# The second of fourteen FFN blocks by seven products instead of plainly, with its weights prepared inside the attention

## The reference

```python
xn = _layernorm(x, axis=-1)                       # x: (2, 512, 512) float32
s = attention(xn, wq, wk, wv, wo)                 # 32 query heads, 8 key heads, window 128
gate_proj = (gate_w - rep(gate_z)) * rep(gate_s)  # (512, 1792), groups of 128 rows; up_proj alike
down_proj = (down_w - rep(down_z)) * rep(down_s)  # (1792, 512)
g = _silu((_silu(xn @ gate_proj) * (xn @ up_proj)) @ down_proj)
return x + s * g
```

## Time and profile before

| | us |
|---|---|
| median of three runs | 873.48 |
| the profiled execution | 873.48 |
| its span, first to last instruction | 871.0 |
| PE busy | 861.2 (99%) |
| DVE busy | 674.5 (77%) |
| POOL busy | 577.2 (66%) |
| ACT busy | 493.5 (57%) |
| mean granted clock of PE | 0.999 of full |
| FFN's first matmul | 663.78 |

### The profile page before, as it was taken

One profiled execution on the slowest core, in us unless ns is written; L12 is line 12 of the kernel. 1 busy time (PEld: TensorE's weight loads), 2 busy tenths in 40 slices (PEclk: granted clock), 3 DMA queues, 4 the chain that ended last, 5 costly groups with the idle time before them and its releaser, 6 DMA issues.

```text
span 871.0 us, 14447 instructions
## 1 busy us (share of the span) xinstructions
PE 861.2 (99%) x4340; PEld 725.6 (83%) x4340; DVE 674.5 (77%) x1264; ACT 493.5 (57%) x1322; POOL 577.2 (66%) x500
## 2 busy tenths in 40 slices
PE   8999999999999999999999999999999999999997
PEld 7888888888888888888888888888888888888886
DVE  8877777877686877877776877778665888989876
ACT  5766565655656566656556555665564444444443
POOL 4665566666675776667666757764446887888865
PEclk9999999999999999999999999999999999999999
DMA  8111110131003012100311020116374564655542
GB/s 263 38 49 37 36 39 25 26 97 36 25 14 106 24 36 90 30 24 24 96 36 36 24 85 24 36 48 159 85 212 120 144 179 132 177 150 167 161 133 96
DMA packets 94851, 72.25 MB, mean 83 GB/s; under 512 B 4192, under 2 KB 80480, under 8 KB 94816
## 3 DMA queue, kind: packets, MB, share of 16 engines
q1 hardware_dynamic: 94096, 70.70, 27.6%
q10 hardware_dynamic: 720, 1.11, 0.4%
HBM read 63.41 MB, written 8.39 MB: 82 GB/s over the span
## 4 chain that ended last, share of the span: by engine, by line
PE 91%; DVE 5%; ACT 2%; DMA 1%; POOL 1%; issue 1%; SPq 0%; DVEq 0%
PE ps L38 29%; PE ps L39 29%; PE ps L40 29%; PE ps L1099 3%; PE ps L1079 1%; ACT probs L1242 1%; DMA work<-L_attn_wv 1%; DVE ps L1507 1%; DMA y<-L_attn_x 0%; DVE work L1503 0%; DVE work L1502 0%; DVE work L1509 0%; POOL w_lo L983 0%; POOL pt_lo L1373 0%; DVE xt_lo L1471 0%
## 5 line engine op out<-in xcount | busy, mean ns | idle before, releaser
L38 PE MATMUL ps<-xt_hi,w_lo 128*128 128x512 f32 x412 | 164.5, 399 | 0.4 <-POOL w_lo L209 0.4
L39 PE MATMUL ps<-xt_lo,w_hi 128*128 128x512 f32 x412 | 161.5, 392 | 0.0
L40 PE MATMUL ps<-xt_hi,w_hi 128*128 128x512 f32 x412 | 160.7, 390 | 0.0
L1373 POOL TENSOR_TENSOR pt_lo<-kept,pt_hi 128x512 fp32r<-128x512 f32 x112 | 142.8, 1293 | 24.9 <-ACT pt_hi L1253 24.6
L1368 POOL TENSOR_TENSOR q_lo<-work,q_hi 128x512 fp32r<-128x512 f32 x63 | 81.3, 1292 | 90.9 <-ACT q_hi L1225 90.9
L1242 ACT ACTIVATE probs<-ps,neg_max 128x128 f32<-128x128 f32 x256 | 90.7, 366 | 42.8 <-DVE neg_max L1527 42.8
L1253 ACT ACTIVATE pt_hi<-kept 128x512 fp32r<-128x512 f32 x112 | 69.2, 633 | 65.6 <-DVE kept L1540 65.6
L38 PE MATMUL ps<-wo_hi,o_lo 128*128 (+1 forms) x256 | 99.8, 390 | 0.1
L40 PE MATMUL ps<-wo_hi,o_hi 128*128 (+1 forms) x256 | 99.6, 389 | 0.0
L39 PE MATMUL ps<-wo_lo,o_hi 128*128 (+1 forms) x256 | 99.6, 389 | 0.0
L40 PEld LDWEIGHTS ps<-xt_hi,w_hi 128*128 128x128 f32 x412 | 77.5, 188 | 17.4
(11 more groups left out here) (174 smaller groups left out, 2234.7 us busy)
## 6 DMA issues: line engine op xcount, KB each, us to landing
work<-L_attn_wq SPq DMA_DIRECT2D x32, 256.0 KB, 2.8
work<-L_attn_wo SPq DMA_DIRECT2D x32, 256.0 KB, 2.7
work<-L_ffn_gate_w SPq DMA_DIRECT2D x14, 256.0 KB, 3.7
work<-L_ffn_gate_z SPq DMA_DIRECT2D x14, 256.0 KB, 4.6
work<-L_ffn_gate_s SPq DMA_DIRECT2D x14, 256.0 KB, 5.8
work<-L_ffn_up_w SPq DMA_DIRECT2D x14, 256.0 KB, 2.9
work<-L_ffn_up_z SPq DMA_DIRECT2D x14, 256.0 KB, 4.0
work<-L_ffn_up_s SPq DMA_DIRECT2D x14, 256.0 KB, 4.5
```

Source lines behind the costliest of these rows:

```text
L38: pe.matmul(out, stat[1], mov[0], start=first, stop=False, skip_group_check=grown)
L39: pe.matmul(out, stat[0], mov[1], start=False, stop=False, skip_group_check=grown)
L40: return pe.matmul(out, stat[0], mov[0], start=False, stop=last, skip_group_check=grown)
L1373: pool.tensor_tensor(pt_lo[:, w, :], kept[:, w, :], pt_hi[:, w, :].bitcast(F32), ALU.subtract).then_inc(pt_split, 1)
```

## The change

- The second block of pair 0 is made by seven products too: `BLOCKS` = 13, `FIRST_BLOCK` = 1, and blk = 0 is now that block. The old numbering moves on by one. Its 48 plain matmuls are replaced by 42.
- blk = 0 has no down products between its own (pair 0 has nothing before it). Its order is U1, U2, S2, S1, S3, G2, S4, and G2 goes to a bank of its own (D = bank 4, a bank that the down products use later), with no wait for the third copy; DVE adds the copy there (`add_gate1`), then ACT takes the silu.
- The last unit of the attention prepares other pieces: down of block 0 at (1, 0), in the row of the token sums' buffer (`first_down`), up of block 1 at (1, 1) and (1, 2), gate at (1, 2), and POOL's `lo_gate(0)` with ACT's two `hi_s` at (1, 3). Before, gate, up and down at (1, 0) to (1, 2).
- ACT's list for blk = 0 is: copy 0, copy 1, hi_up(1), copy 2, hi_gate(1), hi_s(1, 0), silu_gate2, silu_gate1, hi_s(1, 1), hi_down(0). DVE's is: dequantise up(1), add_up1, dequantise gate(1), add_gate2, add_gate1, dequantise down(0).
- At blk = 1 PE waits for the two silus of blk 0 before its first down product.

```diff
-IN_BODY = [(GATE, 1, 0), (UP, 1, 0), (DOWN, 0, 0), (UP, 0, 1), (GATE, 0, 1), (DOWN, 1, 0)]
+IN_BODY = [(DOWN, 0, 0), (UP, 1, 0), (GATE, 1, 0), (UP, 0, 1), (GATE, 0, 1), (DOWN, 1, 0)]
-SEVEN_FROM = 1
-BLOCKS = 2 * (PAIRS - SEVEN_FROM)
+FIRST_BLOCK = 1
+BLOCKS = NI - FIRST_BLOCK
...
-    A, B, C = (0, 3), 1, 2
+    A, B, C, D = (0, 3), 1, 2, 4
...
     def products(self, pe, blk, downs):
...
+        def fifth():
+            if blk:
+                pe.wait_ge(self.seven_mid, 2 * blk)
+            else:
+                pe.wait_ge(sh.silu_done, 2)
+            self.product(pe, blk, S1, self.C, True, self.t_of(T1))
+
+        def sixth():
+            pe.wait_ge(self.copied, 3 * blk + 1)
+            self.product(pe, blk, S2, a, False, self.t_of(T2))
+
+        pe.wait_ge(self.s_split, 2 * blk + 2)
         if blk:
-            pe.wait_ge(self.seven_mid, 2 * blk)
+            fifth()
+            sixth()
         else:
...
+            sixth()
+            fifth()
+
+        if blk == 1:
+
+            pe.wait_ge(self.seven_silu, 2)
...
-        pe.wait_ge(self.copied, 3 * blk + 3)
-        self.product(pe, blk, G2, a, False, self.t_of(T4))
+        if blk:
+            pe.wait_ge(self.copied, 3 * blk + 3)
+            self.product(pe, blk, G2, a, False, self.t_of(T4))
+        else:
+            self.product(pe, blk, G2, self.D, True, self.t_of(T4))
         pe.wait_ge(self.added, 3 * blk + 2)
...
+    def add_gate1(self, dve):
+
+        dve.wait_ge(self.made, self.DONE_P4)
+        dve.wait_ge(self.copied, 3)
+        dve.tensor_tensor(self.bank(self.D), self.bank(self.D), self.copies[:, 2, :], ALU.add).then_inc(self.gate1_added, 1)
...
     def silu_gate1(self, act, blk):
-        act.wait_ge(self.made, 7 * blk + self.DONE_P4)
+        if blk:
+            act.wait_ge(self.made, 7 * blk + self.DONE_P4)
+        else:
+            act.wait_ge(self.gate1_added, 1)
...
-            for e in range(EARLY_PRODUCTS, 4):
-                gate_up(0, e)
             for blk in range(BLOCKS):
+                n, ii = pair_of(blk)
                 def downs(which):
                     for t in which:
-                        down(SEVEN_FROM + blk // 2, 4 * (blk % 2) + t)
+
+                        if n:
+                            down(n, 4 * ii + t)
...
-            sv.hi_up(act, 0)
 
             act.wait_ge(sh.y_ready, NKV * TT)
-            hi_of_mid(0, *ORDER[0])
-            hi_of_mid(0, *ORDER[1])
-            sh.silu(act, 0, 2)
-            sv.hi_gate(act, 0)
-            sv.hi_s(act, 0, 0)
-            sv.hi_s(act, 0, 1)
-            hi_of_mid(0, *ORDER[2])
-            sv.hi_down(act, -1)
-            sh.silu(act, 0, 3)
-            hi_of_mid(0, *ORDER[3])
+            hi_of_mid(0, 0, 0)
+            hi_of_mid(0, 0, 1)
...
+                if blk == 0:
+
+                    sv.copy(act, blk, 1)
+                    sv.hi_up(act, 1)
+                    sv.copy(act, blk, 2)
+                    sv.hi_gate(act, 1)
+                    sv.hi_s(act, 1, 0)
+                    sv.silu_gate2(act, blk)
+                    sv.silu_gate1(act, blk)
+                    sv.hi_s(act, 1, 1)
+                    sv.hi_down(act, blk)
+                    continue
...
-            sv.lo_up(pool, 0)
-            split_mid(0, *ORDER[0])
-            split_mid(0, *ORDER[1])
-            sv.lo_gate(pool, 0)
-            split_mid(0, *ORDER[2])
-            sv.lo_down(pool, -1)
-            split_mid(0, *ORDER[3])
+            split_mid(0, 0, 0)
+            split_mid(0, 0, 1)
...
                 sv.dequantise(dve, blk + 1, GATE)
-                accumulate(n, 4 * ii)
-                accumulate(n, 4 * ii + 1)
-                sv.dequantise(dve, blk, DOWN)
+                for t in (0, 1) if n else ():
+                    accumulate(n, 4 * ii + t)
+                if blk:
+                    sv.dequantise(dve, blk, DOWN)
                 sv.add_gate2(dve, blk)
-                accumulate(n, 4 * ii + 2)
-                accumulate(n, 4 * ii + 3)
+                if blk == 0:
+                    sv.add_gate1(dve)
+                    sv.dequantise(dve, blk, DOWN)
+                for t in (2, 3) if n else ():
+                    accumulate(n, 4 * ii + t)
...
-        FFN_AT = {(0, 3): (-1,), (1, 0): (0,), (1, 1): (1,), (1, 2): (2,)}
+        FFN_AT = {(0, 3): (-1,)}
...
                         hi_of_o(n)
+                        if last and (b, j) == (1, 0):
+                            sh.seven.hi_down(act, -1)
+                        if last and (b, j) == (1, 2):
+
+                            act.wait_ge(scores_ready, UNITS * QB)
+                            sh.seven.hi_up(act, 0)
+                            sh.seven.hi_gate(act, 0)
+                        if last and (b, j) == (1, 3):
+                            for i in range(2):
+                                sh.seven.hi_s(act, 0, i)
...
+                        if last and (b, j) == (1, 0):
+                            sh.seven.lo_down(pool, -1)
+                        if last and (b, j) == (1, 2):
+                            sh.seven.lo_up(pool, 0)
+                        if last and (b, j) == (1, 3):
+                            sh.seven.lo_gate(pool, 0)
...
+                        if last and b == 1 and j < QB - 1:
+                            sh.seven.dequantise(dve, *((-1, DOWN), (0, UP), (0, GATE))[j])
```

More of the change, by code:

```diff
@@ L190, in load_next @@
         wait(eng, sh.scaled, k - sh.RING + 1)
-        self.fetch(eng, s, kind, SEVEN_FROM * 2 + blk)
+        self.fetch(eng, s, kind, FIRST_BLOCK + blk)
     def down_target(self, n, ii):
@@ L364, in index_of, with row @@
         return FfnWeights.index(n, ahead) if ii else FfnWeights.index(n - 1, 3 + ahead)
-    def row(self, kind):
-        return self.gate_row[:, :] if kind == GATE else self.sh.work[:, self.ROW_UP if kind == UP else self.ROW_DOWN, :]
+    def row(self, kind, blk):
+        if kind == GATE and blk:
+            return self.gate_row[:, :]
+        if blk < 0:
+            return self.sh.first_down
+        return self.sh.work[:, self.ROW_UP if kind == UP else self.ROW_DOWN, :]
     def bank(self, i):
@@ L384, in dequantise @@
         else:
-            dve.wait_ge(sh.w_split, FfnWeights.index(SEVEN_FROM - 1, 1) + 1)
-        row = self.row(kind)
+            dve.wait_ge(sh.w_split, FfnWeights.index(0, -1) + 1)
+        row = self.row(kind, blk)
         dve.tensor_tensor(row, w, z, ALU.subtract).then_inc(sh.zero_off, 1)
@@ L421, in lo_up @@
         pool.wait_ge(self.sh.w_hi_done, self.index_of(blk, UP) + 1)
-        self.split(pool, blk, U1, U2, self.row(UP), self.sh.w_split)
+        self.split(pool, blk, U1, U2, self.row(UP, blk), self.sh.w_split)
     def lo_gate(self, pool, blk):
-        sh, up, gate, s = self.sh, self.row(UP), self.row(GATE), self.s
+        sh, up, gate, s = self.sh, self.row(UP, blk), self.row(GATE, blk), self.s
         upper, lower = slice(0, 256), slice(256, 512)
@@ L557, in ffn_block @@
         mid = sh.kept
-        sv = Seven(nc, sh, fw, sb, sem)
+        sv = sh.seven = Seven(nc, sh, fw, sb, sem)
         res = sv.res
@@ L751, in sums @@
             dve.tensor_tensor(sh.y[:, TT - 1, :], ps[:, 7, :], sh.y[:, TT - 1, :], ALU.add)
-            sv.dequantise(dve, 0, GATE)
-            for e in range(EARLY_MIDDLES, 4):
-                dve.wait_ge(mid_split, e - 1)
-                sh.middle(dve, 0, e)
-                if e == EARLY_MIDDLES:
-                    sv.dequantise(dve, -1, DOWN)
             for blk in range(BLOCKS + 1):
-                more, n, ii = blk + 1 < BLOCKS, SEVEN_FROM + blk // 2, blk % 2
+                more, (n, ii) = blk + 1 < BLOCKS, pair_of(blk)
                 if blk:
```

82 lines of the change are left out of this document (36 added, 46 removed).

## The result

The kernel with the change takes 874.81 us (median of 14 runs, 874.5 to 875.37), the kernel before 872.88 (14 runs beside them, 872.33 to 873.61). The ratio is 1.0022, 95% interval 1.0014 to 1.0031: 1.93 us slower. The profiled execution after took 874.56 us with a span of 872.8.

A forecast was written before the change was run, and what follows sets the result against it. PE, busy 99%, was taken as the bound. -1.36 + 0.29 + 0.91 + 1.42 + 0.6 + 4 x 0.12 = +2.3 us (walk: +2.4) gave span 873.4, time 875.9 us (875.0 to 876.6, chance 0.55), range 873.4 to 877.2.

The forecast's parts named there:

- Stop 1: Before S4 of blk 0: PE waits 0.29 us for ACT's copy 2 and DVE's add_gate2.
- Stop 2: Before U2 of blk 1: PE waits 0.91 us for the middle, behind POOL's sums, hi_s and the silus.
- Stop 3: Before the first down product of blk 1: PE waits 1.42 us for POOL's split_mid.
- Stop 4: Before G2 of blk 1: PE waits 0.6 us for ACT's copy, which stands behind hi_s.
- Restarts: On PE after each of the four stops: each restart costs 0.12 us more.
- rival 4: The delay does not heal in blk 2: one more stop of 0.6 to 1.5 us, 877.0 us; chance 0.10.
- rivals 2 and 3: In this order: the work fits, few stops, 872.9 us, chance 0.10; no stops at all, 872.1 us, chance 0.05.
- The table load: At the attention's end on ACT: two hi_s ahead of the silu's table load start it 1.1 us later.
- rival 1: Part of the turns and stops: Stop 3 and Stop 4 shrink to half, +1.0, 874.5 us; chance 0.20.
- The lower bound: Blk 0 and blk 1 if DVE and POOL never wait for each other: -0.6 us, 872.9 us.
- turns: DVE and POOL alternate whole instructions: 1.70 us for both with a 512-wide POOL instruction, 1.15 with a 256-wide one.
- The upper bound: One further turn in each of stops 2 to 4, and a stop in blk 2 as long as Stop 4: +4.

The follow-up runs named there:

- DVE's help: The changed kernel, but DVE instead of POOL makes lo_down(0) and the first mid_lo of blk 0: 874.56 us, ratio 1.0019.
- the first experiment: The changed kernel, but DVE's dequantising of up(1), gate(1) and down(0) takes its second operand from a PSUM bank: 873.46 us, ratio 1.0006.

## Why the prediction was right, point by point

- **The gain on PE** (1.36 us) is there: six matmuls fewer. It is under half of the stops.
- **Stop 1** (0.29): 0.21. The addition ends at 671.59 + 0.51 = 672.10, forecast 672.15.
- **Stop 2** (0.91): 0.83. The forecast had gate(1) ready at 671.16 and the middle's end at 675.90; measured 671.13 and 675.79.
- **Stop 3** (1.42): 1.42. PE starts it at 681.61 of the forecast's count, where the split_mid was forecast for 681.60. DVE's help showed that it hangs on POOL's list: relieved of two instructions, POOL is in time.
- **Stop 4** (0.6): 0.55, by the copy behind hi_s; with the copy first it is gone.
- **Restarts** (0.12 each): 0.07 to 0.11. In all FFN +2.31 us, forecast +2.3 to +2.4. In blk 2 and later no stop appeared, so rival 4 fell; rivals 2 and 3 fell by the stops themselves.
- **The table load** moved by 660.67 + 0.51 - 660.14 = 1.04 us, forecast 1.11. It does set when DVE's list starts: with the load 1.05 us earlier, up(1) started 0.45 us earlier. But moving hi_s to get there gained nothing, since POOL's splits then came later.
- **The time** came out 1.1 us below the forecast: within the range 873.4 to 877.2, but below the 875.0 to 876.6 to which the forecast had given 0.55. 0.7 of the 1.1 lie around the span: I took the 2.5 us of the profiled execution before for both kernels, and the changed one has 1.8. The other 0.4 are the span, 873.4 forecast against a median of 873.0: the profiled execution before, 871.0, stood above the medians of 870.5 to 870.7. The spans are some 2.4 us apart, as forecast. The median is nearer to rival 1's 874.5 than to 875.9, but by chance: rival 1 had stops 3 and 4 at half their size, and they weren't.
- **The bounds.** The lower bound (-0.6, no turns at all) wasn't reached by a run. Without the turns of up(1), gate(1) and down(0) FFN is +0.88 against before, with stops of 0.69 and 0.56 left at the down product and G2(1). I had credited all turns with 3.0 us (875.9 against 872.9); those of three pieces are worth 1.43, and what the turns of up(2), gate(2) and down(1) cost is open. The Trainium skill ("SBUF — State Buffer", section "Who interferes with whom") states that a DVE instruction with two SBUF inputs contends with a GpSimd instruction that reads SBUF. By that rule, the first experiment agrees: 1.53 us with two SBUF inputs, 0.68 with one. Whether the turns explain the rest of the stops, or whether the preparation is too large for the PE work beside it even without turns, no run decides. The upper bound was added up too low by its own words: one further turn in three stops is 3 x 0.45, not 2 x 0.45.
- **The bank of its own** I priced as sparing G2 a wait. It does, 0.85 us, and both times the other stops with their restarts were as much longer.

What stays open is why the projection's start varies by up to 1.4 us between kernels with the same attention, why the time around the span differs between kernels (1.8 us after, 1.9 to 3.1 before), and where the last 0.14 us of the FFN's difference lie.

## What to carry to other kernels

Before work is taken from the bounding engine, read how busy the engines that feed it are in that very stretch: here one was at 97% (POOL 10.52 of 10.88 us), and six matmuls fewer on PE came back as more waiting than they had cost. Stops that hang on one chain don't add up like separate costs: here removing a single one gave from nothing to all of its price back, all of it only at the chain's last link. Nearly all the stops went only when work was spread to idle time and to the other engine and the order was changed too, and even that did no more than undo the loss. And measure a removed wait (here a bank of its own) with the stops behind it, not by itself.

## What was unexpected of the hardware

- DVE and POOL took turns as exactly as worked out: a forecast over 24 us, made of 1.70 us for a pair of 512-wide instructions and 1.15 for a 256-wide one, was met within 0.16 us at each link, the last of them G2(1) at 689.08 against 689.20.
- The relief acts on both sides: with a PSUM operand on DVE, DVE took 0.68 instead of 1.53 us, and POOL 2.54 instead of 2.99 for two instructions.
- A subtraction with int32 input takes turns like one of floats (1.53 and 1.70 us beside POOL, 0.68 alone).
- After each stop PE's first gap is 0.30 to 0.35 us instead of 0.23, at a granted clock of 1.00 over the changed kernel's stretches: some 0.1 us a stop, in stops of 0.12 to 2.30 us alike.
